# Results of the experts scattered to their tokens' rows tile by tile, with the weight and the address carried in each row

## The reference

```python
h = _layernorm(x, axis=-1) * (1 + cb) + sb
router_logits = jnp.einsum('bsh,he->bse', h, gate)             # 8 experts
routing_weights, selected = jax.lax.top_k(router_logits, 2)
routing_weights = jax.nn.softmax(routing_weights, axis=-1)
onehot = jax.nn.one_hot(selected, 8)
tok_w = jnp.einsum('bsk,bske->bse', routing_weights, onehot)
g = jnp.einsum('bsh,ehi->ebsi', h, experts_w1)                 # 128 -> 512
u = jnp.einsum('bsh,ehi->ebsi', h, experts_w3)
eo = jnp.einsum('ebsi,eih->ebsh', silu(g) * u, experts_w2)     # 512 -> 128
x = x + gb * jnp.einsum('ebsh,bse->bsh', eo, tok_w)
```

## Time and profile before

| What | us |
|---|---|
| median of 3 runs | 1269.56 (1268.01 to 1270.36) |
| the profiled execution's own time | 1270.48 |
| its span, first to last instruction | 1268.7 |
| busy in the span: PE / DVE / ACT / POOL | 1087.0 / 852.9 / 535.8 / 591.3 |
| first scatter starts (L586) | 1052.05 |
| first fetch starts (L478) | 1096.98 |
| last copy of a result starts (L720) | 1219.41 |
| first gather starts (L600) | 1222.19 |

### The profile page before, as it was taken

How to read it: one execution, slowest core, us unless ns; L and a number is a source line. 1 busy time by engine, 2 the same in 40 slices (tenths; PEclk the granted TensorE clock), 3 DMA queues, 4 the chain that set the end, 5 groups by cost and what they waited for, 6 DMA issues and landing times.

```text
span 1268.7 us, 16442 instructions
## 1 busy us (share of the span) xinstructions
PE 1087.0 (86%) x5698; PEld 657.3 (52%) x5698; DVE 852.9 (67%) x1659; ACT 535.8 (42%) x1149; POOL 591.3 (47%) x639
## 2 busy tenths in 40 slices
PE   3589999999999999999999999999999840199930
PEld 2356555555555655455555555565555330199930
DVE  3657878776878786777878776878777374044422
ACT  1335544545445454544544545445444412144410
POOL 1725655634545673634645644544453336411136
PEclk9699999999999999999999999999999955599975
DMA  8000000000000000000000000000000061211112
GB/s 226 1 1 1 1 1 1 1 1 1 1 1 1 1 1 1 1 1 2 1 1 1 1 1 1 1 1 1 1 1 1 1 199 35 64 39 49 32 36 76
DMA packets 33088, 24.84 MB, mean 20 GB/s; under 512 B 8816, under 2 KB 28272, under 8 KB 33008
## 3 DMA queue, kind: packets, MB, share of 16 engines
q1 hardware_dynamic: 23664, 17.25, 4.5%
q0 software_dynamic: 2048, 4.20, 1.1%
q10 hardware_dynamic: 7296, 2.36, 0.8%
HBM read 15.54 MB, written 8.26 MB: 19 GB/s over the span
## 4 chain that ended last, share of the span: by engine, by line
PE 74%; DVE 11%; POOL 7%; issue 3%; DMA 2%; ACT 2%; ACTq 1%; POOLq 0%; DVEq 0%
PE PS L1156 19%; PE PS L1110 12%; PE PS L1138 11%; PE PS L1140 9%; PE PS L1221 4%; PE PS L1240 3%; POOL sent L586 3%; PE PS L1086 2%; PE PS L1175 2%; DVE part_max L847 2%; POOL full L600 2%; PE PS L1123 2%; PE PS L1093 2%; PE PS L1166 2%; DVE full L863 2%
## 5 line engine op out<-in xcount | busy, mean ns | idle before, releaser
L847 DVE TENSOR_REDUCE part_max<-PS 128x1 f32<-128x512 f32 (+2 forms) x576 | 340.1, 618 | 132.9 <-PE PS L1110 110.5
L656 ACT ACTIVATE full<-PS 128x512 f32<-128x512 f32 x384 | 223.4, 599 | 198.3 <-PE PS L1140 185.7
L1138 PE MATMUL PS<-rounded 128*128 128x512 f32 (+3 forms) x640 | 271.9, 425 | 5.9 <-ACT diag L665 2.4
L1110 PE MATMUL PS<-rounded 128*128 128x512 f32 (+3 forms) x640 | 250.0, 417 | 2.4 <-DVE V L828 1.3
L533 POOL TENSOR_TENSOR full<-full 128x512 f32<-128x512 f32 x128 | 164.0, 1313 | 156.2 <-PE PS L1156 155.2
L1140 PE MATMUL PS<-rounded 128*128 128x512 f32 (+3 forms) x640 | 233.3, 365 | 0.0
L665 ACT ACTIVATE diag<-PS 128x512 f32<-128x512 f32 (+3 forms) x256 | 111.3, 441 | 214.8 <-PE PS L1143 184.9
L1110 PEld LDWEIGHTS PS<-rounded 128*128 128x128 f32 x640 | 119.7, 193 | 138.2 <-DVE part_max L847 62.9
L561 POOL TENSOR_TENSOR rot_cos<-qkv_sb,cos_sb 128x320 f32<-128x320 f32 x64 | 60.4, 943 | 279.5 <-DVE qkv_sb L825 277.2
L1156 PE MATMUL PS<-full,V 128*64 128x512 f32 x768 | 190.0, 605 | 0.0
L1138 PEld LDWEIGHTS PS<-rounded 128*128 128x128 f32 x640 | 122.9, 192 | 80.8 <-ACT diag L665 27.0
(11 more groups left out here) (140 smaller groups left out, 1439.8 us busy)
## 6 DMA issues: line engine op xcount, KB each, us to landing
full<-in_L_ffn_experts_w_dram SPq DMA_DIRECT2D x16, 256.0 KB, 6.7
sent<-sum_cols SPq DMA_DIRECT2D x1, 2496.0 KB, 19.6
made<-attnT SPq DMA_DIRECT2D x39, 64.0 KB, 1.5
full<-sent SPq DMA_DIRECT2D x9, 256.0 KB, 3.0
out_dram<-XA SPq DMA_DIRECT2D x4, 256.0 KB, 2.4
wqkv<-in_L_attn_Wq_dram ACTq DMA_DIRECT2D x1, 512.0 KB, 4.3
bqkv<-in_L_attn_bq_dram ACTq DMA_DIRECT2D x1, 512.0 KB, 9.8
wo_sb<-in_L_attn_Wo_dram SPq DMA_DIRECT2D x1, 512.0 KB, 8.8
```

The source lines that it names most:

```text
L656: nc.scalar.activation(full[:, k % QUADS, r, :], PS[:, bank, :], ACT.Exp).then_inc(probs_ready, 1)
L847: nc.vector.reduce_max(part_max[:, t, b:b + 1], PS[:, bank, 0:width], AX.X).then_inc(ring_dve, 1)
L1110: last = nc.tensor.matmul(PS[:, bank, 0:w], QT[:, ch % 2, h, t * P:(t + 1) * P], KT[:, 0, keys:keys + w], start=True, stop=not last_bank)
L1138: nc.tensor.matmul(o, KT[:, 0, keys:keys + P], QT[:, ch % 2, h, q0:BANK], start=True, stop=False)
```

## The change

Each row that is scattered to `sent` grows from 128 to 132 words. The four more are `W_FIRST` (the weight of the token's first expert), `W_STEP` (the second's weight less the first's), `FIRST` (the number of the first expert) and `TOKEN` (the token's number). When a quad has been fetched, DVE compares `FIRST` with the tile's expert (`addresses`), and so finds each row's weight (`weight_of`) and its destination (`back_to`: the token for a first choice, 2048 plus the token for a second). ACT's copy of a result becomes a scaled copy, and POOL, in place of SP's write, scatters each tile's 128 rows to `made` as soon as it is copied (`send_back`). An empty slot carries an address of its own behind row 4096, which the clearing of `sent` writes into it; for this the clearing's source is a full 39x132-word area (`blank`) and no longer one repeated tile. `made` is then in token order, so the return is eight plain loads by SP and two DVE adds of 128x512 a chunk. The routing's weight computation moves ahead of the wait for the count. `SLOT_QUADS` goes from 4 to 3.

```diff
-    SLOT_QUADS, Y_ROWS = 4, 8
+    SLOT_QUADS, Y_ROWS = 3, 8
+    ROW = E + 4
+    W_FIRST, W_STEP, FIRST, TOKEN = range(E, ROW)
+    Y_SPACE = 3 * T + SLOT_TILES * P
...
-            sp.wait_ge(pads_ready, 1)
+            sp.wait_ge(blank_ready, 1)
             sp.dma_start(sent.ap().rearrange("(k p) e -> p k e", p=P),
-                         sum_cols[:, 0:E].unsqueeze(1).broadcast_to([P, SLOT_TILES, E])).then_inc(cleared, 16)
+                         blank[:]).then_inc(cleared, 16)
...
-            for q in range(QUADS_OF_SLOTS):
-                for k in quad_tiles(q):
-                    sp.wait_ge(y_copied, k + 1)
-                    sp.dma_start(made.ap()[k * P:(k + 1) * P], y_rows[:, k % Y_ROWS, :]).then_inc(written[k % Y_ROWS], 16)
-                if q + SLOT_QUADS < QUADS_OF_SLOTS:
-                    sp.wait_ge(x_turned, q + 1)
-                    fetch(q + SLOT_QUADS)
+            for q in range(SLOT_QUADS, QUADS_OF_SLOTS):
+                sp.wait_ge(x_turned, q - SLOT_QUADS + 1)
+                sp.wait_ge(back_ready, q - SLOT_QUADS + 1)
+                fetch(q)
+            sp.wait_ge(w13_ready, NX)
+            for k in range(Y_ROWS):
+                sp.wait_ge(written[k], len(range(k, SLOT_TILES, Y_ROWS)) * 16)
+            for ch in range(CHUNKS):
+                for choice in range(2):
+                    first = (choice * TILES + ch * TB) * P
+                    sp.dma_start(returned[:, choice, ch * TB:(ch + 1) * TB],
+                                 made.ap()[first:first + TB * P].rearrange("(i p) e -> p i e", p=P)).then_inc(ld_y[ch], 16)
...
# POOL, start
-            nc.gpsimd.memset(sum_cols[:, 0:E], 0.0)
-            nc.gpsimd.iota(expert_of[:], [[1, SLOT_TILES]], base=0, channel_multiplier=0).then_inc(numbered, 1)
             nc.gpsimd.memset(ones[:], 1.0).then_inc(pads_ready, 1)
+            nc.gpsimd.iota(slot_of[:, 0, :].bitcast(mybir.dt.int32), [[P, TILES]], base=0, channel_multiplier=1)
+            nc.gpsimd.iota(back_to[:].bitcast(mybir.dt.int32), [[P, SLOT_TILES]], base=2 * T, channel_multiplier=1)
+            nc.gpsimd.iota(expert_of[:], [[1, SLOT_TILES]], base=0, channel_multiplier=0)
+            nc.gpsimd.memset(blank[:, :, 0:TOKEN], 0.0).then_inc(numbered, 1)
+            pool.wait_ge(numbered, 1)
+            nc.gpsimd.tensor_copy(blank[:, :, TOKEN], back_to[:].bitcast(mybir.dt.int32)).then_inc(blank_ready, 1)
...
# POOL, scatter and slot loop
-                                                 normed[1][:, t, :], None).then_inc(scattered, 16)
+                                                 rows[:, t, :], None).then_inc(scattered, 16)
...
-            for t in range(TILES):
-                for c in range(2):
-                    nc.gpsimd.indirect_dma_start(returned[:, t, c, :], None, made.ap(),
-                                                 bass.IndirectOffsetOnAxis(ap=slot_of[:, c, t:t + 1], axis=0))\
-                      .then_inc(gathered[t // TB], 16)
+            def send_back(k):
+                pool.wait_ge(y_copied, k + 1)
+                pool.wait_ge(back_ready, k // TB + 1)
+                nc.gpsimd.indirect_dma_start(made.ap(), bass.IndirectOffsetOnAxis(ap=back_to[:, k:k + 1], axis=0),
+                                             y_rows[:, k % Y_ROWS, :], None).then_inc(written[k % Y_ROWS], 16)
+
+            split_rows(0)
+            for k in range(SLOT_TILES):
+                if k >= 2:
+                    send_back(k - 2)
+                if k % TB == 1 and k // TB + 1 < QUADS_OF_SLOTS:
+                    split_rows(k // TB + 1)
+            send_back(SLOT_TILES - 2)
+            send_back(SLOT_TILES - 1)
...
# ACT, y_out
-                nc.scalar.copy(y_rows[:, k % Y_ROWS, :], PS[:, 5 + k % 2, 0:E]).then_inc(y_copied, 1)
+                act.wait_ge(back_ready, k // TB + 1)
+                nc.scalar.activation(y_rows[:, k % Y_ROWS, :], PS[:, 5 + k % 2, 0:E], ACT.Copy,
+                                     scale=weight_of[:, k:k + 1]).then_inc(y_copied, 1)
...
# DVE, between the ranks and the wait for the count (L956)
+            nc.vector.tensor_copy(rows[:, :, TOKEN], slot_of[:, 0, :].bitcast(mybir.dt.int32))
+            dve.wait_ge(exp_logits, 1)
+            link(nc.vector.scalar_tensor_tensor(out=tok_w[:], in0=rank[:], scalar=1.5, in1=tok_w[:],
+                                                op0=ALU.is_lt, op1=ALU.mult))
+            nc.vector.reduce_sum(tok_sum[:], tok_w[:], AX.X)
+            for c, table in ((0, tok_w[:]), (1, numbers[:, 0:NX].unsqueeze(1).broadcast_to([P, TILES, NX]))):
+                last = nc.vector.scalar_tensor_tensor(out=picked[:, c], in0=rank[:], scalar=0.0, in1=table,
+                                                      op0=ALU.is_equal, op1=ALU.mult)
+            link(last)
+            link(nc.vector.tensor_reduce(place_of[:].rearrange("p c t -> p (c t)"),
+                                         picked[:].rearrange("p c t x -> p (c t) x"), AX.X, ALU.add))
+            nc.vector.tensor_copy(rows[:, :, FIRST], place_of[:, 1])
+            nc.vector.scalar_tensor_tensor(out=tok_pair[:, 1], in0=place_of[:, 0], scalar=-2.0, in1=tok_sum[:],
+                                           op0=ALU.mult, op1=ALU.add)
+            link(nc.vector.reciprocal(tok_sum[:], tok_sum[:]))
+            nc.vector.tensor_tensor(rows[:, :, W_FIRST], place_of[:, 0], tok_sum[:], ALU.mult)
+            link(nc.vector.tensor_tensor(rows[:, :, W_STEP], tok_pair[:, 1], tok_sum[:], ALU.mult))
             dve.wait_ge(counted, 1)
...
# DVE, slot loop: addresses(0) ahead of it, addresses(k // TB + 1) at every k % TB == 1
+            def addresses(q):
+                dve.wait_ge(fetched[q % SLOT_QUADS], (q // SLOT_QUADS + 1) * 16)
+                tiles = slice(quad_tiles(q)[0], quad_tiles(q)[-1] + 1)
+                at = q % SLOT_QUADS * TB
+                tail = [slots[:, at:at + len(quad_tiles(q)), k] for k in (W_FIRST, W_STEP, FIRST, TOKEN)]
+                link(nc.vector.tensor_tensor(other[:, tiles], tail[2], owner_of[:, tiles], ALU.not_equal))
+                link(nc.vector.tensor_tensor(weight_of[:, tiles], other[:, tiles], tail[1], ALU.mult))
+                nc.vector.tensor_tensor(weight_of[:, tiles], weight_of[:, tiles], tail[0], ALU.add)
+                nc.vector.scalar_tensor_tensor(out=back_to[:, tiles], in0=other[:, tiles], scalar=float(T), in1=tail[3],
+                                               op0=ALU.mult, op1=ALU.add).then_inc(back_ready, 1)
...
# DVE, return
-                dve.wait_ge(gathered[ch], 2 * TB * 16)
-                for c in range(2):
-                    for i in range(ch * TB, (ch + 1) * TB):
-                        last = nc.vector.scalar_tensor_tensor(
-                            out=XA[:, i, :], in0=returned[:, i, c, :], scalar=tok_pair[:, c, i:i + 1],
-                            in1=XA[:, i, :], op0=ALU.mult, op1=ALU.add)
+                dve.wait_ge(ld_y[ch], 32)
+                link(nc.vector.tensor_tensor(of_chunk(XA, ch), of_chunk(XA, ch), of_chunk(returned[:, 0], ch), ALU.add))
+                nc.vector.tensor_tensor(of_chunk(XA, ch), of_chunk(XA, ch), of_chunk(returned[:, 1], ch), ALU.add)\
+                  .then_inc(y_added, 1)
```

More of the change, by code:

```diff
@@ L378, in block_kernel @@
         owner = bqkv[:].rearrange("p g n -> p (g n)")[:, 0:SLOT_TILES * NX].rearrange("p (k x) -> p k x", x=NX)
-        owner_sum = bqkv[:].rearrange("p g n -> p (g n)")[:, SLOT_TILES * NX:SLOT_TILES * (NX + 1)]
+        owner_sum, owner_of, weight_of = (bqkv[:].rearrange("p g n -> p (g n)")[:, SLOT_TILES * k:SLOT_TILES * (k + 1)]
+                                          for k in range(NX, NX + 3))
+        other_at = SLOT_TILES * (NX + 3)
+        other = bqkv[:].rearrange("p g n -> p (g n)")[:, other_at:other_at + SLOT_TILES]
         mask16 = sb("mask16", [P, TILES, NX], BF16)
@@ L420, in block_kernel @@
         written = [sem("written%d" % k) for k in range(Y_ROWS)]
-        gathered = [sem("gathered%d" % k) for k in range(CHUNKS)]
+        back_ready, ld_y = sem("back_ready"), [sem("ld_y%d" % k) for k in range(CHUNKS)]
         y_added = sem("y_added")
@@ L919, in _ @@
             for x in n.order:
-                if x == ("rowsum", 0):
-                    dve.wait_ge(cleared, 16)
                 if x == ("rowsum", GROUPS * N_J - 1):
@@ L1012, in hidden_out @@
                   .then_inc(hidden_copied, 1)
+            addresses(0)
             for k in range(SLOT_TILES):
@@ L1021, in _, with of_chunk @@
                     hidden_out(k - 1)
+                if k % TB == 1 and k // TB + 1 < QUADS_OF_SLOTS:
+                    addresses(k // TB + 1)
             hidden_out(SLOT_TILES - 1)
+            def of_chunk(t, ch):
+                return t[:, ch * TB:(ch + 1) * TB].rearrange("p a b -> p (a b)")
             for ch in range(CHUNKS):
-                dve.wait_ge(gathered[ch], 2 * TB * 16)
-                for c in range(2):
-                    for i in range(ch * TB, (ch + 1) * TB):
```

(10 more changed lines are left out.)

59 lines of the change are left out of this document (28 added, 31 removed).

## The result

The changed kernel takes 1239.72 us (median of 4 runs, 1238.14 to 1241.08) against 1269.41 us: ratio 0.9767, 95% interval 0.9749 to 0.9784, so 29.7 us less. A second measurement later, five runs, gave 1239.41 us, ratio 0.9756 [0.9743, 0.9770]. The forecast was 1238.2 us, range 1233 to 1246.

What follows compares the result with a forecast made beforehand. The prediction took PE to bound attention and the slot loop, and 32 POOL gathers the return. Terms -32.3 + 0 + 1.1 + 0.3 + 0.1 - 0.6 = -31.4 took 1269.56 to 1238.2 us, range 1233 to 1246.

Steps and rivals of the forecast that it cites:

- The return: From last copy to end: 49.0 us with 32 POOL gathers becomes 16.7, so -32.3, between -34 and -28.5.
- All six terms: New tail after the last copy: scaled copy 0.1, POOL wake 0.3, scatter 2.2, loads 9.9, adds 1.4, last write 2.8.
- The load term: Eight 256 KB loads at the end: 9.9 us, 8.9 to 10.9, at 1.0 a load set by the engines' rate.
- The slot loop: Loop over 39 result tiles: PE bounds it, so the added POOL scatters and small DVE instructions cost 0.
- Rival 1: Slot loop: scatters lock DVE out, time 1294, or 1256 with unslowed scatters; 4 in 100, 2 of them slower.
- rival 2: Slot loop: DVE starves the scatters and POOL bounds the loop at 2.96 us a slot, 1245; 8 in 100.
- The rule that the forecast tied to rival 2: Slot loop: a two-port DVE copy holds ports shared with GpSimd until it ends, blocking descriptors; 2.96 us a slot.
- Routing: Between ranks and `slot_of`: eleven DVE instructions take 2.4 us, 1.31 was idle, so +1.1, between 0 and 1.9.
- First scatters: The 32 scatters after `slot_of`: some slowed beside DVE's long subtractions, +0.3, between -3 and +4.
- Rows of 528 bytes: First stage: 32 scatters keep their number of rows, first fetch 3% larger, +0.1, at most 1.0.
- rival 3: First stage: a 132-word row costs two descriptors, 31 us more on the path, 1269; 3 in 100.
- The start: Before attention: the later 2.5 MB clearing lets ACT's loads finish earlier, -0.6, between -1.6 and +1.5.

Runs made afterwards that it cites:

- experiment 9: Changed kernel with tokens numbered by partition, so each return load reads pieces of 2048 bytes instead of 512: 1238.43 us, ratio 0.9743.
- Experiments 1: Changed kernel with SP writing the slot loop's results plainly in slot order, no scatter in the loop: 1238.14 us, ratio 0.9758.
- 3: Changed kernel with each result tile scattered twice, the second time to a spare tensor: 1240.86 us, ratio 0.9783.
- 8: Changed kernel with DVE's eight long subtractions of expert weights beside the first scatters cut into 64 of 128 columns: 1247.92 us, ratio 0.9831.
- 6: Changed kernel with POOL's eight multiplications of w2 held back until DVE's last normalisation is done: 1240.81 us, ratio 0.9776.
- 7: Changed kernel without POOL's multiplications of w2; DVE multiplies the gate in when copying results from PSUM, replacing ACT's copy: 1234.07 us, ratio 0.9704.
- Experiment 5: Changed kernel with the clearing of the slot tensor issued only when ACT's eight loads have landed: 1236.42 us, ratio 0.9744.

## Why the forecast held, step by step

**The return, -32.3; measured -32.0,** and -32.3 in the second profile. All six terms were in the right place. In forecast and measurement: copy with a scale 0.1 (0.37 instead of 0.27), POOL wakes 0.3 (0.27), scatter to SP 2.2 (2.37), eight loads 9.9 (10.2, then 9.86), two adds 1.4 (1.42), last write 2.8 (2.7). The load term was the largest and came from four fetches alone; that each further load would cost 1.0 us is what the second profile shows: chunks of two loads are added 2.66, 1.81 and 1.62 us apart, 6.1 for six. The reason that was given, the transfer engines' rate, fits their busy share there (1.07); experiment 9 excludes SP's issue.

**The slot loop, 0; measured +0.6 and -0.5 in two profiles, 0 to within that spread.** Experiments 1 and 3 show it: without scatters, with 39 and with 78, transposes to last copy take 119.19, 118.96 and 118.88 us. Rival 1 (a scatter locks DVE out) and rival 2 (DVE starves the scatters, POOL bounds the loop) fall together: scatters of 964 ns, and DVE's L1067 at 688 ns. The rule that the forecast tied to rival 2 (the Trainium skill, SBUF — State Buffer, Who interferes with whom) speaks of the copy alone. With only L1011 waited out, POOL would need 0.97 + 0.69 + 0.30 + 0.31 = 2.27 us a slot, under PE's 2.79, so the forecast priced this rule too high. The choice in the forecast, to read L1011's 0.69 us as a form that doesn't take the shared path, was right. The mutual hold that the earlier trace rows show is real, but it needs a DVE instruction that reads two operands from SBUF (8) or POOL's own two-operand arithmetic (6, 7), and the loop has neither beside a scatter at any length. It does have short ones: the four small instructions of `addresses` read two SBUF operands each, and once in four tiles they stand beside a scatter (1158.63 to 1159.26, the scatter 1158.23 to 1159.19), which stays at 0.96 us.

**Routing, +1.1; measured +0.94.** The eleven instructions took 2.3 us (forecast 2.4), and L1010 read the counts right behind them.

**First scatters, +0.3; measured +0.24** between the first and the last start, in part by luck. The forecast had L1004 (L1041 now) start about as far into the scatters as before; it starts 0.95 us behind the first (1054.32 against 1053.37), where it was 2.97. So three took 1.96 to 1.97 us as before, and a fourth 1.53, some 0.6 more. The rest took 0.96 instead of 0.97, which gives half of that back; no term of the forecast had this. Rows of 528 bytes at +0.1, shows in scatters of 0.96 us: rival 3 (two descriptors a row) fails, since 32 of them are no longer than with 512 bytes. The first fetch to the transposes took 3.01 instead of 2.99.

**The start, -0.6; measured -0.1,** and +0.8 in the second profile. This is the term that was mis-sized. The forecast followed ACT's queue, which did come free 0.8 us earlier in the first profile (17.48 instead of 18.24) but not in the second (18.31); the path to the first matmul went over DVE and the landing of `sin_sb` (27.39 before, then 27.28 and 28.19). In the ten profiles with the early clearing the first matmul stands at 29.02 to 29.98, and at 29.13 in the one of before: no gain that can be told. Experiment 5 shows that about 1.7 us was there.

**The total.** -29.8 measured by the spans against -31.4. The 1.6 between them is attention and the loop (+1.1), where the clock was lower, and the start term (+0.5); what is left cancels. The second profile, without the dip at 87 us, is 32.4 us under before. The mechanism is confirmed term by term; that the total came within 1.6 and 1.0 of -31.4 is no finer than the spread of the executions allows.

## What to carry to other kernels

If a gather at the end is issued row by row because rows come back in the wrong order, send each result to its place as it is made, on a queue that is idle then, and read back plainly: the 39 us of gathers gave way to 1 us at a join and 10 us of loads. Before two engines' work is put side by side ask what each reads: the same scatter costs 0.96 us beside copies from PSUM and up to 12 beside a dense row of short two-operand instructions on SBUF. When an instruction is slow beside another, moving it may only change its victim (6); removing it paid (7).

## What the runs showed of the hardware

- A POOL scatter is starved more by a dense row of short DVE instructions with two SBUF operands than by a few long ones: 1.97 us beside subtractions that start 1.15 us apart, 12.02 beside 64 that start 0.20 apart. Four short ones by themselves (`addresses`) leave it at 0.96.
- POOL's multiply over 128x512 stretches DVE's comparisons of 0.2 to 0.35 us to 0.93 to 1.47 us, about its own 1.25 us (six of the seven beside it; one stayed at 0.32).
- An indirect transfer of 128 rows takes 0.96 us and a gap of 0.30 on POOL, scatter and gather, for rows of 512 and of 528 bytes; it is over 2.4 us after its start.
- Eight loads of 256 KB in pieces of 512 bytes, issued in 5.0 to 6.3 us, take 9.6 to 10.4 us over all runs here, and the first six of them 8.0 to 8.9. In pieces of 2048 bytes, issued in 3.7 us, the first six take 8.7.
- The same program's granted clock can dip in the midst of attention, 0.74 instead of 1.00 from 87 to 90 us, and 1.5 us are lost by it.
